# One tile step of a scan-and-experts kernel, reordered: the residual and the output bias are summed ahead of the output product, and dt's clamp, two small vector forms and the convolution's silu change their chunk

## The reference, cut to what matters

```
x = x + attn_a(layernorm(x))     # selective scan, below
x = x + ffn(layernorm(x))        # 16 experts, 6 of them with a weight
x = x + attn_b(layernorm(x))
x = x + ffn(layernorm(x))

attn_a(x):                                   # d_inner 512, 16 states
    xn = layernorm2(x);  x_in, z = split(xn @ in_proj.T + b)
    x_conv = silu(conv4(x_in) + conv_b)
    B, C   = split(x_conv @ x_proj.T + b)
    delta  = clip(softplus(x_conv @ dt_proj.T + b), 1e-4, 10)
    per row t:  h = exp(clip(delta*A, -10, 0)) * h + delta*B*x_conv
                every 16th row: h scaled so that its norm is at most 10
                y = sum_n C[n]*h[n] + D*x_conv
    out = (y * silu(z)) @ out_proj.T + out_b
    return layernorm2(x + out) * alpha + beta
```

## Time and profile before

| what | value |
|---|---|
| median of 3 runs | 4960.72 us |
| profiled execution | 4964.46 us, its span 4962.7 us |
| first scan to the last one of the first stage | 79.0 to 3229.2 us, 512 scans in 64 tiles |
| busy in the span | PE 88%, DVE 78%, ACT 59%, POOL 54% |
| busy from 1200 to 1800 us | DVE 550 of 600 us, PE 548, POOL 508, ACT 471 |
| granted TensorE clock | 0.953 of full speed over the span |

### The profile page before, as it was taken

How to read it: one execution, slowest core, us unless ns; L and a number is a source line. 1 busy time by engine, 2 the same in 40 slices (tenths; PEclk the granted TensorE clock), 3 DMA queues, 4 the chain that set the end, 5 groups by cost and what they waited for, 6 DMA issues and landing times.

```text
span 4962.7 us, 83401 instructions
## 1 busy us (share of the span) xinstructions
PE 4378.3 (88%) x22592; PEld 3072.6 (62%) x22592; DVE 3858.7 (78%) x9556; ACT 2914.2 (59%) x8578; POOL 2690.9 (54%) x1412
## 2 busy tenths in 40 slices
PE   5789998989898999898989898876777779999999
PEld 4777777777777777777777777644434444444444
DVE  4899999999999999999999999943333357777776
ACT  5777777777777777777777777624444421111111
POOL 3888888888888888888888888800000000000000
PEclk8999999999999999999999999988888889999999
DMA  2111111111111111111111111100101100000000
GB/s 91 58 52 50 51 51 51 50 51 51 50 52 48 53 47 54 48 54 48 54 48 54 48 52 50 43 31 26 51 25 38 34 25 19 17 19 19 17 19 16
DMA packets 119271, 212.96 MB, mean 43 GB/s; under 512 B 19232, under 2 KB 85664, under 8 KB 118560
## 3 DMA queue, kind: packets, MB, share of 16 engines
q1 hardware_dynamic: 119072, 211.10, 13.0%
HBM read 184.83 MB, written 26.21 MB: 43 GB/s over the span
## 4 chain that ended last, share of the span: by engine, by line
PE 39%; DVE 19%; issue 18%; POOL 15%; ACT 7%; DMA 1%; DVEq 1%; SPq 1%; POOLq 0%; ACTq 0%
PE ps L649 22%; POOL prod L348 8%; POOL hb L356 6%; PE ps L626 5%; ACT zr L413 4%; DVE macc L962 3%; DVE selp L949 3%; PE ps L776 3%; PE ps L755 2%; DVE xcv L1068 1%; PE ps_dA L776 1%; PE ps L679 1%; DVE hb L886 1%; DVE nrs L877 1%; PE ps_dA L755 1%
## 5 line engine op out<-in xcount | busy, mean ns | idle before, releaser
L649 PE MATMUL ps<-w_x,mxT 128*128 128x512 f32 x4096 | 1876.7, 596 | 9.6 <-DVE macc L962 9.6
L869 DVE TENSOR_TENSOR_SCAN hb<-ps_dA,hb 128x1088 f32<-128x1088 f32 x512 | 1240.8, 2423 | 111.2 <-POOL hb L356 101.4
L348 POOL TENSOR_TENSOR prod<-hb,cbc 128x1024 f32<-128x1024 f32 x512 | 1121.6, 2191 | 259.7 <-DVE hb L888 259.7
L356 POOL TENSOR_TENSOR hb<-u,bbc 128x1024 f32<-128x1024 f32 x512 | 1201.7, 2347 | 84.1 <-POOL prod L348 72.1
L413 ACT ACTIVATE zr<-dt,aneg 128x128 f32<-128x128 f32 x4096 | 1234.1, 388 | 0.7 <-DVE dt L1024 0.7
L626 PEld LDWEIGHTS ps<-prod,ident 128*128 128x128 f32 x8192 | 1025.0, 205 | 295.1 <-POOL prod L348 235.4
L626 PE MATMUL ps<-prod,ident 128*128 128x128 f32 x8192 | 1043.1, 290 | 183.6 <-POOL prod L348 183.6
L962 DVE SCALAR_TENSOR_TENSOR macc<-ps,gate,macc 128x256 f32<-128x256 f32 x2048 | 977.9, 477 | 271.4 <-PE ps L649 208.2
L649 PEld LDWEIGHTS ps<-w_x,mxT 128*128 128x128 f32 x4096 | 736.7, 191 | 701.0 <-issue 647.0
L422 ACT ACTIVATE ps_dA<-zr 128x1024 f32<-128x1024 f32 x512 | 517.0, 1010 | 0.0
L429 ACT ACTIVATE sq<-hb 128x64 f32<-128x64 f32 x512 | 158.1, 309 | 476.0 <-DVE hb L869 472.8
(11 more groups left out here) (184 smaller groups left out, 5196.7 us busy)
## 6 DMA issues: line engine op xcount, KB each, us to landing
bbc<-bcd SPq DMA_DIRECT2D x128, 512.0 KB, 3.7
cbc<-bcd SPq DMA_DIRECT2D x128, 512.0 KB, 3.5
xt<-in_x SPq DMA_DIRECT2D x128, 128.0 KB, 3.1
x2d<-macc SPq DMA_DIRECT2D x64, 128.0 KB, 1.7
xcv<-x2d SPq DMA_DIRECT2D x64, 128.0 KB, 2.1
x3d<-x1b SPq DMA_DIRECT2D x64, 128.0 KB, 1.8
x1b<-x3d SPq DMA_DIRECT2D x64, 128.0 KB, 2.0
out_dram<-macc SPq DMA_DIRECT2D x64, 128.0 KB, 1.7
```

The costliest lines, as they stand in the source:

```text
L348: TT(dst, states, cc, ALU.mult).then_inc(M["prodp"], 1)
L356: TT(hb[c % 2][:].rearrange("p (e n) s -> p e n s", e=EB)[:, :, :, 1:SL], u[k][:, :, t0:t0 + CH].rearrange("p e (n s) -> p e n s", n=1).br ...
L649: last = mm(banks[p % len(banks)][:], mxT[k][:, j, :], w_x[:, j, p * 512:(p + 1) * 512], start=(j == 0), stop=(j == KD - 1))
L869: V.tensor_tensor_scan(states, dA, states, 0.0, ALU.mult, ALU.add).then_inc(M["scan"], 1)
```

## The change

In the first stage, by part:

1. **Back (B) on DVE.** Before, chunk 2 had `oo = x*r1 + product` and then `oo += bias`, and chunk 3 the statistics. Now chunk 1 has `oo = x*r1 + bias` (behind `halfway(1)`), chunk 2 has `oo += product` and the statistics, chunk 3 the rest of the norm (`se3`, `r3`, `o3`), which stood in chunk 4. `se3` reads `sd3`, which ACT makes in its chunk 3. PE's skip product, which overwrites the product's bank, now waits for `o2` in place of `o1`.
2. **POOL.** Times alpha and plus beta go from chunk 6 to chunk 4; plus x stays in chunk 6.
3. **dt.** The clamp goes from the end of chunk 1 to the end of chunk 0. The four bias passes for it go from chunk 0 to the end of chunk 7 of the step before, and ACT's two softplus passes with them. The B/C bias pass `bcv` goes the other way, from chunk 7 to chunk 0 of the next step, and SP's `bcd` store with it: it now stands right ahead of the wait for it and of the load of `bbc[0]`.
4. **Router.** `selp` goes from the end of chunk 7 to the end of chunk 5; the steps behind it are each one later, and the semaphore's counts follow.
5. **ACT.** The convolution's silu goes from chunk 5, ahead of the decays, to chunk 4, behind them. `DECAYS` gives 6, 7, 6, 11, 7, 13, 14, 0 decays to the chunks in place of 0, 8, 9, 12, 14, 9, 12, 0.

```
-DECAYS = (0, 0, 8, 17, 29, 43, 52, 64, 64)
+DECAYS = (0, 6, 13, 19, 30, 37, 50, 64, 64)
...
                 if "G" in stages:
+                    sp.wait_ge(M["bcv"], AHEAD + i + 2)
+                    sp.dma_start(bcd[1 - k].rearrange("h w n t -> (w n) h t"),
+                                 bcv[:].rearrange("r (h t) -> r h t", h=2)).then_inc(M["bcd"], 16)
                     sp.wait_ge(M["bcd"], AHEAD + (i + 2) * 16)
...
-                if c == 6 and "B" in stages:
+                if c == 4 and "B" in stages:
                     g.wait_ge(M["o3"], AHEAD + i)
                     TT(oo[:], oo[:], ga_row[:], ALU.mult).then_inc(M["o4"], 1)
                     g.wait_ge(M["o4"], AHEAD + i)
                     TT(oo[:], oo[:], be_row[:], ALU.add).then_inc(M["o5"], 1)
+                if c == 6 and "B" in stages:
                     g.wait_ge(M["o5"], AHEAD + i)
...
+                        if F:
+                            a.wait_ge(M["dtb"], AHEAD + (i + 3) * EB)
+                            act(dtt[:], dtt[:], ACT.Exp).then_inc(M["edt"], 1)
...
                     if G_ and DECAYS[c] < DECAYS[c + 1]:
                         decays(i + 1, 1 - k, DECAYS[c], DECAYS[c + 1])
+                    if c == 4 and F:
+                        a.wait_ge(M["xcc"], AHEAD + i + 3)
+                        a.wait_ge(M["sz"], AHEAD + (i + 2 if G_ else 0))
+                        act(sg[:], xcv[k][:], ACT.Exp, scale=-1.0).then_inc(M["ex"], 1)
...
-                        pe.wait_ge(M["o1"], AHEAD + (i if B else 0))
+                        pe.wait_ge(M["o2"], AHEAD + (i if B else 0))
...
+                if G_:
+                    v.wait_ge(M["ldt"], AHEAD + i + 2)
+                    v.wait_ge(M["zr"], AHEAD + i + 1)
+                    v.wait_ge(M["u"], AHEAD + i + 1)
+                    TS(dt[:], dtt[:], 1e-4, 10.0, ALU.max, ALU.min).then_inc(M["dt"], 1)
                 end(0)
...
+                    STT(oo[:], xt[1][:], r1b[1 - k][:], ob_row[:], ALU.mult, ALU.add).then_inc(M["o1"], 1)
                 end(1)
...
-                    STT(oo[:], xt[1][:], r1b[1 - k][:], YP[:, 0:D], ALU.mult, ALU.add).then_inc(M["o1"], 1)
                     v.wait_ge(M["o1"], AHEAD + i)
-                    TT(oo[:], oo[:], ob_row[:], ALU.add).then_inc(M["o2"], 1)
-                end(2)
...
+                    TT(oo[:], oo[:], YP[:, 0:D], ALU.add).then_inc(M["o2"], 1)
...
+                if B:
+                    v.wait_ge(M["sd3"], AHEAD + i)
+                    TS(sc[:, 11:12], sc[:, 10:11], 1e-6, None, ALU.add).then_inc(M["se3"], 1)
```

More of the change, by code:

```diff
@@ L476, in step @@
                         norms(i, c)
[L477 to L481, removed]
                     if c == 1:
@@ L531, in step @@
                             route_norm(i - 1)
+                        if F:
+                            a.wait_ge(M["dtb"], AHEAD + (i + 3) * EB)
+                            act(dtt[:], dtt[:], ACT.Exp).then_inc(M["edt"], 1)
+                            a.wait_ge(M["edt"], AHEAD + i + 3)
+                            act(dtt[:], dtt[:], ACT.Ln, bias=1.0).then_inc(M["ldt"], 1)
                         if X_:
@@ L997, in step @@
                 if G_:
[L998 to L1002, removed]
+                    v.wait_ge(M["bc"], AHEAD + i + 2)
+                    v.wait_ge(M["bcd"], AHEAD + (i + 1) * 16)
+                    TS(bcv[:], F1[0:RB, XP:XP + P], b_xp[:], None, ALU.add).then_inc(M["bcv"], 1)
                 halfway(0)
@@ L1053, in step @@
                     TS(sc[:, 8:9], mv[:, 2, 1:2], D / (D - 1.0), 1e-19, ALU.mult, ALU.max).then_inc(M["vc3"], 1)
+                end(2)
+                start(3)
+                if X_:
+                    route_scores(i - 2, k, F1)
+                halfway(3)
+                if B:
+                    v.wait_ge(M["sd3"], AHEAD + i)
+                    TS(sc[:, 11:12], sc[:, 10:11], 1e-6, None, ALU.add).then_inc(M["se3"], 1)
+                if F:
+                    v.wait_ge(M["xi"], AHEAD + i + 3)
+                    v.wait_ge(M["carry"], AHEAD + i + 3)
+                    TT(xin[:, :, TAPS - 1:], bank4(F0), bias4(b_in[:, 0:EB]), ALU.add).then_inc(M["xib"], 1)
+                if B:
+                    v.wait_ge(M["se3"], AHEAD + i)
+                    V.reciprocal(sc[:, 12:13], sc[:, 11:12]).then_inc(M["r3"], 1)
+                    v.wait_ge(M["r3"], AHEAD + i)
+                    TS(oo[:], oo[:], mv[:, 2, 0:1], sc[:, 12:13], ALU.subtract, ALU.mult).then_inc(M["o3"], 1)
                 end(3)
@@ L1086, in step @@
                     last.then_inc(M["zb"], 1)
-                router(5, 6)
                 if L_:
@@ L1090, in step @@
                     V.bn_stats(st[:, 0, :], xt[0][:]).then_inc(M["st1"], 1)
+                router(5, 6)
                 end(5)
@@ L1116, in step @@
                 if F:
-                    v.wait_ge(M["bc"], AHEAD + i + 3)
-                    v.wait_ge(M["bcd"], AHEAD + (i + 2) * 16)
-                    TS(bcv[:], F1[0:RB, XP:XP + P], b_xp[:], None, ALU.add).then_inc(M["bcv"], 1)
+                    v.wait_ge(M["dtp"], AHEAD + i + 3)
+                    v.wait_ge(M["dt"], AHEAD + (i + 2 if G_ else 0))
+                    for e in range(EB):
+                        TS(dtt[:, e, :], F0[:, e * P:(e + 1) * P], b_dt[:, e:e + 1], 40.0, ALU.add, ALU.min)\
+                            .then_inc(M["dtb"], 1)
                 if L_:
```

71 lines of the change are left out of this document (18 added, 53 removed).

## The result

Seven runs of the changed kernel gave 4973.57 to 4979.03 us, median 4976.18, beside a median of 4960.52 (7 runs) for the kernel before: ratio 1.0035, 95% interval 1.0024 to 1.0047. It is slower by 16 us, where 4831 had been forecast, outside the range of 4795 to 4905. The profiled execution took 4979.03, its span 4977.2.

The account below looks back on a forecast made before the run. No engine was taken as full: DVE, PE and POOL hand work to and fro, DVE and POOL leading in turn. Gains of 0.78 and 1.32 make 2.10 us a tile, 130 us over 62 tiles: 4831, range 4795 to 4905.

Parts of the forecast that it names:

- T1: Start of scan(1), counted from the tile's first scan; forecast at 6.01 us, where it was 5.66.
- Chunk 0, the clamp at 0.35: On DVE, the clamp of dt moved into chunk 0 would cost 0.35 us, since POOL holds nothing there.
- Chunk 1, the sum held to the end of inputs(2), and DVE first: DVE's residual-and-bias sum waits for POOL's inputs(2), then precedes POOL's u, making u 0.28 us later; chance 0.52.
- the rival by which POOL keeps its turn: A ready POOL instruction goes ahead of DVE's waiting one in chunks 1 and 5; 4901 us, chance 0.20.
- T3 by POOL, only 0.27 of the bias addition had: Scan(3) starts at 17.20 us, set by POOL; of the bias addition's 2.04 us only 0.27 is gained.
- Chunk 3, the root 1.47 behind the sum of squares: DVE's `se3` waits for ACT's square root, ready 1.47 us behind the sum; scan(4) comes at 24.11, before 23.28.
- DVE's idle wait in it: Sign in chunk 3: DVE waits 1.3 to 1.4 us for ACT's root before `se3`.
- Chunks 4 to 7 on POOL, 16.87 from prod(3) to scan(7) without a wait: POOL runs unbroken for 16.87 us, so scan(7) starts at 41.19 in place of 41.97, gaining 0.78 a tile.
- Chunk 7, 1.32 less: On DVE, subtraction and B/C pass leave, dt passes and a router step come: 1.32 us a tile less.
- chunk 7 at 6.4 to 6.6 us: Sign in DVE's timeline: the tile's last chunk would last 6.4 to 6.6 us.
- The 6% given to "slower": Chance 0.06 that the changed kernel is slower, all of it from ACT's root coming late; 5035 us.
- a late root: Rival: ACT's root passes come behind its 11 decays, DVE stands 4.8 us in chunk 3; 5035 us, chance 0.06.

Follow-up runs that it names:

- e6_shift12: Changed kernel with 12 of DVE's idle semaphore increments issued behind its loop in place of ahead of it; median 4863.5 us, ratio 0.9803.
- e12_bias: The changed kernel with the 12-increment shift, old residual put back in chunk 2 with the bias added behind it; median 4946.8 us, ratio 0.9972.
- after: The changed kernel as forecast, against the kernel before, with no follow-up edit; median 4976.18 us, ratio 1.0035.
- e10_selp: The changed kernel with the 12-increment shift, router's subtraction put back from chunk 5 to its old place in chunk 7; median 4856.6 us, ratio 0.9791.

## Why the prediction was wrong, step by step

The steps of the way to scan(7), in us from the tile's start, against the tile of e6_shift12 above:

| | T1 | T2 | T3 | T4 | T7 | next T0 |
|---|---|---|---|---|---|---|
| forecast | 6.01 | 11.52 | 17.20 | 24.11 | 41.19 | 47.82 |
| e6_shift12 | 6.00 | 11.50 | 17.08 | 23.87 | 40.85 | 48.37 |

- *Chunk 0, the clamp at 0.35*: right.
- *Chunk 1, the sum held to the end of inputs(2), and DVE first*: right. The sum took 1.23, and u shows the 0.2 us as length (1.47 against 1.27). So POOL's next instruction, though ready, let the waiting one of DVE through; the rival by which POOL keeps its turn is refuted here and in chunk 5, where the subtraction ended with inputs(6).
- *T3 by POOL, only 0.27 of the bias addition had*: right in T3. But e12_bias shows the sum to be worth 83 us once the statistics stand behind it: the forecast's row of gains gives the parts in an order, and the worth of a part alone is another thing.
- *Chunk 3, the root 1.47 behind the sum of squares*: its mechanism was right, its size 1.35 (1485.99 to 1487.34); DVE's idle wait in it was 1.13, where 1.3 to 1.4 had been named.
- *Chunks 4 to 7 on POOL, 16.87 from prod(3) to scan(7) without a wait*: right, 16.86 (1489.06 to 1505.92), and `xcv` waited for nothing. In after itself POOL does wait, as told above, behind the loop's stand.
- *Chunk 7, 1.32 less*: this step failed. The subtraction left, but the hold didn't: "together 1.32 less" priced the denominator at its time of before. Scan(7) comes earlier now, POOL's inputs(0') begins earlier against DVE's small work, and the first form that can be held pays. I took the hold away with the instruction that showed it, while it belongs to the moment. The chunk lost 0.45 us in the mean (7.73 to 7.28) in place of 1.32. Cost: 55 us.
- *What the forecast didn't have at all*: the branch back. It spoke of "chunk 7 at 6.4 to 6.6 us" and T0 right behind it; the step from there to the next pass of the loop was taken over from before with its 0.2, where it is 3.8 at every second tile. Cost: 113 us. This is the step that put the time outside the range: with the loop in place the changed kernel took 4863.5 us, inside it.

In sum: 4831, less 27 (scan(7) 0.43 a tile earlier than forecast in the mean, times 62), and 55 for the denominator make 4859, where e6_shift12 measured 4864; with 113 for the loop-back it is 4972, where 4976 was measured. The 55 and the 113 are themselves differences between runs, so only the 27 is tested by this sum. The 6% given to "slower" rested on a late root, which isn't in the trace: the sign came out on its side by something that no rival named.

What stays open: that a page is 128 instructions and three may be used is inferred from eight places of one loop and the size of the packets; no run moved ACT's body (314 instructions at 687 to 1001 before; if its borders lay at the same counts it would touch four pages, which would fit its 2.5 us), nor looked for the exact border. Why the stall is 2.8 us at one place and 3.8 at another isn't explained. Why e10_selp lost nothing, where 0.2 us a tile were to be lost, is only partly followed: chunk 5 is 0.24 shorter, chunk 6 0.25 longer and chunk 7 0.10 shorter.

## What to carry to other kernels

When a change adds even two instructions inside or ahead of a hardware loop, read the rows of the loop's own branch on every engine, and the packets of the instruction queue, before and after: an engine that already waits at its branch shows the price, and a few idle instructions moved across the loop tell whether it is the place. A hold between DVE and POOL belongs to the moment, not to the instruction that shows it: when one held operation is moved away, look at which form stands in the same moment next, and write small ones so that they take one tensor from SBUF. With the accident of the loop's place taken out, this change is worth 97 us (4960.5 to 4863.5); with it, it measured as a loss of 16.

## What the hardware showed that was not expected

- A loop body of 367 or 369 instructions on DVE costs 2.7 to 4.2 us at each branch back, or 0.2, by its place alone; moving that of the kernel before by 11 places cost 115 us, 2.4% of the program.
- `scalar_tensor_tensor` on 128 x 1 with two operands from SBUF is held by a running POOL instruction like a large one (1.10 us); `tensor_scalar` with the same two operands, the second as scalar for each partition, took 0.20 beside the same POOL instruction. The Trainium skill, SBUF — State Buffer, "Who interferes with whom", says that a DVE instruction with two SBUF inputs contends with a POOL instruction that reads SBUF; this trace agrees, for one number a partition (1.10 us) as for 256 (1.23).
- `tensor_scalar` from SBUF to SBUF on 128 x 256 was held (1.43 against 0.41), that on 128 x 1 was not (0.20).
